# Router rows turned back by TensorE and copied by ScalarE, and a step width summed in PSUM, in a state-space stage

## The chip, the cores and the metric

The kernel runs on one core of a Trainium2 chip. The metric is the device time of one execution in microseconds (us), smaller is better. The core's engines are TensorE (PE, its weight loads are PEld), VectorE (DVE), ScalarE (ACT), GpSimd (POOL) and SyncE (SP, which only issues DMAs). Each engine works through its own program in order; semaphores order the engines among each other. Everything is float32 unless a row says bf16.

## The reference

Two layers over x of shape 2 x 1024 x 128 (2048 rows in all). Layer 0 is adaptive layer norm, a selective state-space block (256 channels, 16 states), a gated residual, a second adaptive norm and a mixture of 8 experts. Layer 1 is the same frame around a gated scan and 16 experts. The change touches the state-space block and the norm behind it:

```python
mod = (_silu(L0_c) @ L0_wmod).reshape(L0_c.shape[0], 6, 1, -1)
sa, ca, ga, sb, cb, gb = (mod[:, 0], mod[:, 1], mod[:, 2], mod[:, 3], mod[:, 4], mod[:, 5])
h = _layernorm(x, axis=-1) * (1 + ca) + sa
...
xc = jax.nn.silu(xc)
x_dbl = jnp.einsum('bld,ed->ble', xc, W_x)
dt, Bm, Cm = jnp.split(x_dbl, [R, R + N], axis=-1)
dt = jax.nn.softplus(jnp.einsum('blr,dr->bld', dt, W_dt) + b_dt)
A = -jnp.exp(A_log)
A_bar = jnp.exp(dt[..., None] * A)
Bu = dt[..., None] * Bm[:, :, None, :] * xc[..., None]
...
_, h_all = jax.lax.associative_scan(comb, (A_bar, Bu), axis=1)
y = jnp.einsum('bldn,bln->bld', h_all, Cm) + D_param * xc
y = y * jax.nn.silu(z)
return jnp.einsum('bld,ed->ble', y, W_out)
...
x = x + ga * _L0_attn_ref(h, ...)
h = _layernorm(x, axis=-1) * (1 + cb) + sb
x = x + gb * _L0_ffn_ref(h, ...)
```

Below, `dt` is called the step width, `dt * xc` is u, the second `h` is "the router's rows": the router scores them and the experts read them from HBM.

## The kernel before, in words

**The stage.** The 2048 positions are cut into 4 chunks of 512 (c = 0 to 3; an even chunk begins a sequence, an odd one goes on from saved carries). Channels are two halves d of 128 partitions. A chunk has 16 steps, one for each state n; step g = 16 c + n. For each step ScalarE writes the decays exp(dt * A) of both halves into PSUM (`decays`), GpSimd multiplies `bu = uT * b` over 128 x 1024 (`inputs`), VectorE runs one scan for each half (`scan`), and the states are multiplied by C into `prod`: of even steps by VectorE (`products`, out of PSUM), of odd steps by GpSimd (`products` of that engine, out of SBUF). TensorE adds `prod` into two PSUM banks with an identity (`add_up`). GpSimd's order is inputs(2k), inputs(2k+1), products(2k-1). `bu` and `prod` are rings of 4 steps, and the B and C rows rings of 3 pairs, which SyncE loads. So for each pair of steps GpSimd has three multiplications, VectorE four scans and one multiplication.

**The work around it** is placed by hand in tables `before` (the next chunk's preparation) and `after` (the chunk behind it), one for each engine, keyed by n, or by the pair m of a chunk for TensorE. For the next chunk: convolution (`conv`, `conv_copy`), `silus`, `low_rows` and `low_and_rows`, `dt_rows`, `dt_parts` and `dt_logs` (softplus in parts: dtT holds relu, a PSUM bank the logarithm), then on VectorE `dt_and_u` at n = 11 and 12, and the z half (`z_half`, `z_copy`). For the chunk behind: `gate_y` at n = 2, `project_out`, `add_x` with its moments at n = 6, `rstd`, `inverse_std` at n = 9 (line 1493), `normed_rows` (ScalarE writes x-hat to `h_tok`), `rows_back` (TensorE turns it into columns), `columns_out` (ScalarE scales and shifts the columns into `hR`), `score_first` (router scores from `hR`), and `router_rows`: at n = 15 VectorE does the same scaling and shifting on the rows themselves, two operations on 128 x 512 (lines 1478 and 1479), for chunks 0, 1 and 2. Chunk 3's rows are done by GpSimd after the stage. `save_rows` (SyncE) writes the rows to HBM.

**Banks.** PSUM bank FRONT serves in turn conv, low rows, the step width of half 0 and z; bank BACK the step width of half 1, the output projection, the turned rows and the scores. FRONT is the bank that the change gives one more use.

The stage spans about 48.7 us (the first `bu`) to 287.6 us. What follows it is the choice of experts and layer 0's experts, then layer 1.

## Time and profile before

| | |
|---|---|
| median of 3 runs (lowest, highest) | 717.08 us (714.65, 719.17) |
| the profiled execution's own time | 712.0 us |
| its span, first to last instruction | 710.2 us |
| mean granted TensorE clock (share of 2.4 GHz) | 0.809 |
| busy share of the span: PE, DVE, ACT, POOL | 64%, 67%, 47%, 58% |

The profile is of one execution; its own time is 5.1 us under the median of the others. Busy shares are means over stages that have different limits, so they say little of one stage: there the rows of each engine in order of time are to be read.

### The profile page before, as it was taken

To read this page: it belongs to the slowest core of one execution; us is meant where nothing else is said; L and a number is where in the kernel's file an instruction comes from. 1 tells how busy PE (TensorE), PEld (TensorE's weight loads), DVE (VectorE), ACT (ScalarE), POOL (GpSimd) and SP (SyncE) were. 2 spreads that over 40 slices of the span, in tenths; PEclk is the share of its full clock that TensorE was granted. 3 is DMA by queue.
4 is the path that set the end of the run, shared out by engine and by line. 5 is a ranking of instruction groups with operands and counts; after the bars stand their busy time and mean duration, and the time that the engine had idled before them with its cause. 6 is when DMAs were issued, how large, how long until landed. Compare 5 with 4: busy or idle time off the path is not lost.

```text
span 710.2 us, 8170 instructions
## 1 busy us (share of the span) xinstructions
PE 456.9 (64%) x2119; PEld 309.4 (44%) x2119; DVE 477.3 (67%) x910; ACT 335.6 (47%) x652; POOL 414.0 (58%) x321
## 2 busy tenths in 40 slices
PE   3655976968787477635878678069640387787520
PEld 2222332423333233524767677025540277776510
DVE  5958899999899999771333223637633747767817
ACT  3164855774586264111222224276320079689805
POOL 0029999999899899216666644421475200645850
PEclk9887999999899799856889989559655589999865
DMA  5053656554344450014666664400011645634125
GB/s 184 0 181 110 182 172 205 176 178 133 119 152 148 134 177 31 15 37 145 197 195 202 194 159 129 122 0 0 16 45 37 208 162 178 212 135 149 42 67 154
DMA packets 58382, 90.21 MB, mean 127 GB/s; under 512 B 7569, under 2 KB 32658, under 8 KB 58338
## 3 DMA queue, kind: packets, MB, share of 16 engines
q1 hardware_dynamic: 51010, 78.36, 34.8%
q0 software_dynamic: 5024, 10.30, 4.7%
q10 hardware_dynamic: 2304, 1.05, 0.5%
q8 instruction: 18, 0.29, 0.2%
q14 instruction: 26, 0.21, 0.1%
HBM read 66.21 MB, written 11.14 MB: 109 GB/s over the span
## 4 chain that ended last, share of the span: by engine, by line
PE 18%; DVE 10%; ACT 10%; issue 7%; another core or an unknown queue 7%; POOL 4%; DMA 3%; ACTq 2%; SPq 1%; DVEq 0%; POOLq 0%
PE ps L1257 5%; PE ps L1246 4%; POOL y_dram L549 2%; PE ps L1415 1%; ACTq L962 1%; PE ps L1297 1%; ACT freq L1002 1%; ACT mag L1000 1%; ACT mag L986 1%; ACT fabs L993 1%; ACT fabs L977 1%; POOL prod L589 1%; PE ps L1086 1%; DMA y_dram<-ys,rows_i 1%
## 5 line engine op out<-in xcount | busy, mean ns | idle before, releaser
L578 POOL TENSOR_TENSOR bu<-uT,b_sb 128x1024 f32<-128x1024 f32 x64 | 151.3, 2386 | 29.5 <-DVE uT L1760 29.5
L549 POOL DMA_INDIRECT y_dram<-ys,rows_i x86 | 92.9, 1080 | 115.9 <-DVE ys L2015 64.2
L1142 PE MATMUL ps<-prod,cst 128*128 128x512 f32 x256 | 128.6, 649 | 39.9 <-DVE yT L1794 16.4
L762 ACT ACTIVATE ps<-dtT,neg_a 128x512 f32<-128x512 f32 x128 | 83.3, 683 | 39.7 <-DVE prod L1784 27.3
L1142 PEld LDWEIGHTS ps<-prod,cst 128*128 128x128 f32 x256 | 50.4, 205 | 109.8 <-issue 75.5
L589 POOL TENSOR_TENSOR prod<-hs,c_sb 128x1024 f32<-128x1024 f32 x32 | 77.7, 2430 | 11.7 <-DVE hs L1774 5.9
L1257 PE MATMUL ps<-w_s,ht 128*128 x312 | 48.6, 305 | 26.2 <-issue 11.0
L859 ACT ACTIVATE ht<-ps,b1T 128x128 f32<-128x128 f32 x78 | 24.5, 368 | 85.9 <-PE ps L1246 48.4
L1257 PEld LDWEIGHTS ps<-w_s,ht 128*128 128x128 f32 x312 | 43.3, 215 | 30.7 <-issue 30.7
L1415 PE MATMUL ps<-xt,mfr 128*128 128x128 f32 x376 | 51.6, 293 | 4.5 <-DVE freq L1978 3.0
L1848 DVE TENSOR_SCALAR ht<-ps,b1T 128x128 f32<-128x128 f32 x78 | 23.8, 346 | 44.8 <-PE ps L1246 26.0
L540 POOL DMA_INDIRECT xl<-h_dram,rows_i x39 | 37.8, 969 | 27.0 <-DVE rows_i L1684 15.4
L1415 PEld LDWEIGHTS ps<-xt,mfr 128*128 128x128 f32 x376 | 48.8, 208 | 6.4 <-issue 4.6
L1246 PE MATMUL ps<-xt,w1r 128*128 128x128 f32 x312 | 48.0, 305 | 1.4 <-issue 1.4
L1246 PEld LDWEIGHTS ps<-xt,w1r 128*128 128x128 f32 x312 | 44.8, 221 | 1.5 <-issue 1.5
L1784 DVE TENSOR_TENSOR prod<-ps,c_sb 128x1024 f32<-128x1024 f32 x32 | 39.2, 1225 | 3.3 <-issue 0.4
L645 POOL DMA_INDIRECT x_slots<-h_tok,slot_i x32 | 32.1, 1004 | 14.3 <-issue 9.8
L1858 DVE TENSOR_TENSOR ys<-ps,b_s 128x128 f32<-128x128 f32 x39 | 11.3, 290 | 42.9 <-remote 19.1
L1116 PE MATMUL ps<-hT,wconv 128*128 128x512 f32 x64 | 34.1, 685 | 9.2 <-ACT zsT L706 8.5
L1774 DVE TENSOR_TENSOR_SCAN ps<-ps,bu 128x512 f32<-128x512 f32 x32 | 37.3, 1210 | 4.1 <-ACT ps L762 4.0
L1774 DVE TENSOR_TENSOR_SCAN ps<-ps,carry,bu 128x512 f32<-128x512 f32 x32 | 39.2, 1270 | 0.6 <-ACT carry L774 0.3
L1774 DVE TENSOR_TENSOR_SCAN hs<-ps,carry,bu 128x512 f32<-128x512 f32 x32 | 39.2, 1266 | 0.1
(289 smaller groups left out, 908.7 us busy)
## 6 DMA issues: line engine op xcount, KB each, us to landing
b_sb<-b_rows SPq DMA_DIRECT2D x32, 512.0 KB
c_sb<-b_rows SPq DMA_DIRECT2D x32, 512.0 KB
mfr<-mf_s SPq DMA_DIRECT2D x47, 256.0 KB
w1r<-in_w SPq DMA_DIRECT2D x39, 256.0 KB
mf_s<-in_mf SPq DMA_DIRECT2D x16, 256.0 KB
xl<-x_slots SPq DMA_DIRECT2D x47, 64.0 KB
w_s<-in_w SPq DMA_DIRECT2D x9, 256.0 KB, 4.8
down_s<-in_down SPq DMA_DIRECT2D x16, 128.0 KB
```

Of the source, the lines that this page charges most:

```text
L540: pool.indirect_dma_start(xl0[:, j % (2 * XR), :], None, h_dram, bass.IndirectOffsetOnAxis(ap=rows_i[:, 0, j:j + 1], axis=0)).then_inc(loa ...
L549: pool.indirect_dma_start(y_dram[l], bass.IndirectOffsetOnAxis(ap=rows_i[:, 1, j:j + 1], axis=0), ys[:, j % slots, :], None).then_inc(save ...
L578: nc.gpsimd.tensor_tensor(bu[:, g % RING, :, :], uT[:, c % 2, :, :], b_sb[:, k % BRING, g % 2, :].unsqueeze(1).broadcast_to([P, ND, CHUNK] ...
L589: nc.gpsimd.tensor_tensor(prod[:, g % RING, :, :], hs[:, k % HRING, :, :], c_sb[:, k % CRING, 1, :].unsqueeze(1).broadcast_to([P, ND, CHUNK]),
L762: nc.scalar.activation(decay_of(g, d), dtT[:, c % 2, d, :], ACT.Exp, scale=neg_a[:, d, n:n + 1]).then_inc(S["a_ready"], 1)
L1116: last = nc.tensor.matmul(bank(conv_bank(c, d)), wconv[:, k, d * P:(d + 1) * P], hT[:, b, lo + k:lo + k + CHUNK], start=k == 0, stop=k == ...
L1142: last = nc.tensor.matmul(bank(Y_BANK + d), ident, prod[:, g % RING, d, :], start=n == 0, stop=n == NS - 1)
L1246: last = nc.tensor.matmul(ps[:, b, at:at + P], w1r[:, j % WR, k * P:(k + 1) * P], xt0[:, j % 2, :], start=True, stop=True)
L1257: last = nc.tensor.matmul(ps[:, 6 + j % 2, 0:C], ht0[:, j % 2, k * P:(k + 1) * P], w2_s[:, bass.ds(e, 1), k, :].rearrange("p a c -> p (a c ...
L1415: last = nc.tensor.matmul(ps[:, b + p % 2 * 2, at:at + P], mfr[:, j % (2 * MR), row:row + P], xt1[:, p % 2, j % 2 * P:(j % 2 + 1) * P], st ...
L1774: nc.vector.tensor_tensor_scan(out, decay_of(g, d), bu[:, g % RING, d, :], carry[:, d, n:n + 1] if c % 2 else 0.0, ALU.mult, ALU.add).then ...
L1784: nc.vector.tensor_tensor(prod[:, g % RING, :, :], even_states(), c_sb[:, k % CRING, 0, :].unsqueeze(1).broadcast_to([P, ND, CHUNK]), ALU. ...
```

## The change

1. **Router's rows.** VectorE's `router_rows` is gone for chunks 0 to 2. In its place TensorE turns `hR` back into rows (`rows_forth`, four transposes into bank FRONT) and ScalarE copies the bank to `h_tok` (a new `router_rows`, one copy of 128 x 512). For chunk 0 this happens in chunk 2 (TensorE at pair m = 2, ScalarE at n = 6), for chunk 1 at the same places of chunk 3, for chunk 2 right after the loop, ahead of the last `project_out`. Waits are added for the bank: TensorE's `low_rows` of chunk 3 waits for the first copy, the last `project_out` for the third, and `columns_out` waits for `rows_ps0` before it overwrites `hR`. SyncE saves the rows of chunks 0 and 1 at n = 14 of chunks 2 and 3 and not at n = 4.
2. **Step width.** In `dt_and_u` the sum goes to the PSUM bank and not to `dtT`, and u is multiplied out of the bank: each of VectorE's two operations then has one operand in SBUF and one in PSUM. ScalarE gets a new `dt_copy` (PSUM to `dtT`, 128 x 512) for each half and chunk: at n = 12 and 13, and two ahead of the first decays. What waited for `dt_ready` because of the bank or because of `dtT` (decays, `z_half`, `project_out`, `rows_back`) now waits for `dt_copied`; GpSimd's `inputs` and ScalarE's `dt_parts` still wait for `dt_ready`.
3. **Small moves.** `z_copy` of half 0 goes from n = 13 to n = 14. Two small loads count on another semaphore.

(The list of semaphore names is left out of the diff.)

```diff
@@ -400,8 +400,8 @@
                 later += [(w2_s[:, es, :, :], w2[:, es, :, :], "in_w1")]
-            later += [(b2_s[:, :, :], b2.partition_broadcast(P), "in_w1"), (nw_s[:, :], norm_w.partition_broadcast(P), "in_nw"),
-                      (rb1_s[:, :], rbias1.partition_broadcast(P), "in_nw"), (b1_r[:, :], b1.rearrange("e (k p) -> (e k) p", p=P), "in_b1"),
+            later += [(b2_s[:, :, :], b2.partition_broadcast(P), "in_w1"), (nw_s[:, :], norm_w.partition_broadcast(P), "in_l1"),
+                      (rb1_s[:, :], rbias1.partition_broadcast(P), "in_l1"), (b1_r[:, :], b1.rearrange("e (k p) -> (e k) p", p=P), "in_b1"),
                       (phase_r[:, :], phase.rearrange("e (k p) -> (e k) p", p=P), "in_b1")]
@@ -431,7 +431,7 @@
                         sp.dma_start(dst, src).then_inc(S[done], 16)
-                    if n == 4 and c >= 2:
+                    if n == 14 and c >= 2:
                         save_rows(c - 2)
@@ -748,11 +748,16 @@
 
+            def dt_copy(c, d):
+
+                act.wait_ge(S["dt_ready"], 2 * c + d + 1)
+                nc.scalar.activation(dtT[:, c % 2, d, :], bank(dt_bank(d)), ACT.Copy).then_inc(S["dt_copied"], 1)
+
             def decays(g):
...
                 if n == 0:
-                    act.wait_ge(S["dt_ready"], 2 * c + 2)
+                    act.wait_ge(S["dt_copied"], 2 * c + 2)
                 for d in range(ND):
@@ -786,11 +791,18 @@
                     act.wait_ge(S["logit_ps"], c)
+                    act.wait_ge(S["rows_ps0"], c)
                 b = c // 2
...
 
+            def router_rows(c):
+
+                act.wait_ge(S["rows_ps0"], c + 1)
+                nc.scalar.activation(h_tok[:, c * CT:(c + 1) * CT, :].rearrange("p t c -> p (t c)"), bank(FRONT), ACT.Copy).then_inc(S["h_ready"], 1)
+
             before = {2: lambda c: conv_copy(c, 0), 4: lambda c: conv_copy(c, 1), 7: low_and_rows, 9: lambda c: dt_parts(c, 0),
-                      11: lambda c: dt_logs(c, 1), 13: lambda c: z_copy(c, 0), 15: lambda c: z_copy(c, 1)}
+                      11: lambda c: dt_logs(c, 1), 12: lambda c: dt_copy(c, 0), 13: lambda c: dt_copy(c, 1), 14: lambda c: z_copy(c, 0),
+                      15: lambda c: z_copy(c, 1)}
             after = {8: lambda c: rstd(1, c), 12: normed_rows, 14: columns_out}
@@ -804,6 +816,8 @@
             columns_first(3)
+            dt_copy(0, 0)
+            dt_copy(0, 1)
             act.wait_ge(S["modT_ps"], 1)
@@ -824,11 +838,14 @@
                     silus(c + 1)
+                if n == 6 and c >= 2:
+                    router_rows(c - 2)
                 if n == 10 and c + 1 < NCHUNK:
...
                     after[n](c - 1)
+            router_rows(NCHUNK - 2)
             after[8](NCHUNK - 1)
@@ -1098,7 +1115,7 @@
                 if d == 0 or c == 0:
-                    pe.wait_ge(S["dt_ready"], 2 * c + d + 1)
+                    pe.wait_ge(S["dt_copied"], 2 * c + d + 1)
                 else:
@@ -1120,6 +1137,8 @@
                 pe.wait_ge(S["xc_ready"], c + 1)
+                if c + 1 == NCHUNK:
+                    pe.wait_ge(S["h_ready"], NCHUNK + 1)
                 for d in range(ND):
@@ -1149,7 +1168,9 @@
                 if c + 1 < NCHUNK:
-                    pe.wait_ge(S["dt_ready"], 2 * c + 4)
+                    pe.wait_ge(S["dt_copied"], 2 * c + 4)
+                else:
+                    pe.wait_ge(S["h_ready"], NCHUNK + c)
                 if c and c + 1 < NCHUNK:
@@ -1162,12 +1183,25 @@
                 if c + 2 < NCHUNK:
-                    pe.wait_ge(S["dt_ready"], 2 * c + 6)
+                    pe.wait_ge(S["dt_copied"], 2 * c + 6)
                 if c + 1 == NCHUNK:
...
                 last.then_inc(S["hT_ps"], 1)
+
+            def rows_forth(c):
+
+                pe.wait_ge(S["hT_sb"], NCHUNK + c + 1)
+                if c == 0:
+                    pe.wait_ge(S["xc_raw"], 2 * NCHUNK)
+                elif c == 1:
+                    pe.wait_ge(S["z_raw"], 2 * NCHUNK)
+                else:
+                    pe.wait_ge(S["h_ready"], NCHUNK + c)
+                for t in range(CT):
+                    last = nc.tensor.transpose(ps[:, FRONT, t * P:(t + 1) * P], hR[:, t * P:(t + 1) * P], ident)
+                last.then_inc(S["rows_ps0"], 1)
 
@@ -1198,6 +1232,8 @@
                     after[m](c - 1)
+                if m == 2 and c >= 2:
+                    rows_forth(c - 2)
                 if m == NS // 2 - 1:
@@ -1215,6 +1251,7 @@
                     score_first(c - 1)
+            rows_forth(NCHUNK - 2)
             project_out(NCHUNK - 1)
@@ -1493,11 +1530,6 @@
 
-            def router_rows(c):
-
-                dve.wait_ge(S["hT_ps"], NCHUNK + c + 1)
-                modulate(c, CB, SB)
-
             def moments(c, done):
@@ -1756,8 +1788,8 @@
                 dve.wait_ge(S["softp_done"], 2 * c + d + 1)
-                then(nc.vector.tensor_tensor(dtT[:, q, d, :], dtT[:, q, d, :], bank(dt_bank(d)), ALU.add))
-                nc.vector.tensor_tensor(uT[:, q, d, :], dtT[:, q, d, :], xcT[:, q, d, :], ALU.mult).then_inc(S["dt_ready"], 1)
+                then(nc.vector.tensor_tensor(bank(dt_bank(d)), dtT[:, q, d, :], bank(dt_bank(d)), ALU.add))
+                nc.vector.tensor_tensor(uT[:, q, d, :], bank(dt_bank(d)), xcT[:, q, d, :], ALU.mult).then_inc(S["dt_ready"], 1)
 
@@ -1803,7 +1835,7 @@
             before = {11: lambda c: dt_and_u(c, 0), 12: lambda c: dt_and_u(c, 1)}
-            after = {2: gate_y, 6: add_x, 9: inverse_std, 15: router_rows}
+            after = {2: gate_y, 6: add_x, 9: inverse_std}
             norm_scale(3)
@@ -1860,7 +1892,7 @@
 
-                dve.wait_ge(S["in_l1"], 32)
+                dve.wait_ge(S["in_l1"], 64)
                 dve.memset(inner_f[:, :], 0.0)
@@ -1945,7 +1977,6 @@
             gated_scan(3)
-            dve.wait_ge(S["in_nw"], 32)
             best_second(0)
```

## Rows read from the trace of the kernel before

**Rows 1.** Busy time of PE, PEld, DVE, ACT, POOL, 46 to 289 us; granted clock, DMA share, GB/s.

```profile
46.00:289.00 243.00, 186.59 (x444) 81.80 (x445) 229.54 (x220) 139.43 (x244) 227.16 (x96) 0.89 0.47 150
```

**Rows 2.** GpSimd's groups of instructions, 48 to 289 us: count, busy us, mean ns, idle before.

```profile
L578 POOL TENSOR_TENSOR bu<-uT,b_sb 128x1024 f32<-128x1024 f32 x64 | 151.3, 2386 | 29.5 <-DVE uT L1760 29.5
L589 POOL TENSOR_TENSOR prod<-hs,c_sb 128x1024 f32<-128x1024 f32 x32 | 77.7, 2430 | 11.7 <-DVE hs L1774 5.9 <-PE ps L1142 4.5 <-DVE ps L1774 1.2
```

**Rows 3.** VectorE's groups of the same stretch.

```profile
L1479 DVE TENSOR_TENSOR h_tok<-h_tok,mod 128x512 f32<-128x512 f32 x3 | 8.1, 2716 | 0.1
...
L1493 DVE SCALAR_TENSOR_TENSOR ln_nmr<-ln_mv,ln_rs 128x4 f32<-128x4 f32 x3 | 4.3, 1441 | 0.0
L1478 DVE TENSOR_TENSOR h_tok<-h_tok,mod 128x512 f32<-128x512 f32 x3 | 4.3, 1438 | 0.0
...
L1794 DVE TENSOR_TENSOR yT<-ps,zsT 128x1024 f32<-128x1024 f32 x3 | 3.6, 1214 | 0.0
```

**Rows 4.** The line of u's multiplication: ns min/median/max, first and last start.

```profile
L1760 DVE TENSOR_TENSOR uT<-dtT,xcT x8: 691/826/2382, 45.4 to 218.5; 128x512 f32<-128x512 f32 x8
```

**Rows 5.** GpSimd in order of time: start, us, line, count, idle before.

```profile
88.48 2.35 POOL L589 TENSOR_TENSOR prod<-hs,c_sb 128x1024 f32<-128x1024 f32 x1
...
95.42 2.79 POOL L589 TENSOR_TENSOR prod<-hs,c_sb 128x1024 f32<-128x1024 f32 x1
98.17 5.10 POOL L578 TENSOR_TENSOR bu<-uT,b_sb 128x1024 f32<-128x1024 f32 x2
...
167.16 2.79 POOL L589 TENSOR_TENSOR prod<-hs,c_sb 128x1024 f32<-128x1024 f32 x1
...
176.44 2.35 POOL L589 TENSOR_TENSOR prod<-hs,c_sb 128x1024 f32<-128x1024 f32 x1 [1.42 <-DVE hs L1774]
...
192.91 2.38 POOL L589 TENSOR_TENSOR prod<-hs,c_sb 128x1024 f32<-128x1024 f32 x1 [2.33 <-PE ps L1142]
...
275.80 4.67 POOL L578 TENSOR_TENSOR bu<-uT,b_sb 128x1024 f32<-128x1024 f32 x2
...
284.89 2.65 POOL L589 TENSOR_TENSOR prod<-hs,c_sb 128x1024 f32<-128x1024 f32 x1 [2.12 <-PE ps L1142]
```

**Rows 6.** VectorE in order of time, first half.

```profile
53.40 2.35 DVE L1774 TENSOR_TENSOR_SCAN ps<-ps,bu 128x512 f32<-128x512 f32 x2
...
84.88 2.33 DVE L1774 TENSOR_TENSOR_SCAN hs<-ps,bu 128x512 f32<-128x512 f32 x2
...
90.68 2.33 DVE L1774 TENSOR_TENSOR_SCAN hs<-ps,bu 128x512 f32<-128x512 f32 x2
...
132.88 0.69 DVE L1800 TENSOR_TENSOR x_tok<-x_tok,ps 128x512 f32<-128x512 f32 x1
...
135.01 2.46 DVE L1774 TENSOR_TENSOR_SCAN hs<-ps,carry,bu 128x512 f32<-128x512 f32 x2
```

**Rows 7.** VectorE in order of time, the end.

```profile
276.27 2.45 DVE L1774 TENSOR_TENSOR_SCAN hs<-ps,carry,bu 128x512 f32<-128x512 f32 x2
...
282.31 2.45 DVE L1774 TENSOR_TENSOR_SCAN hs<-ps,carry,bu 128x512 f32<-128x512 f32 x2
...
293.51 0.69 DVE L1800 TENSOR_TENSOR x_tok<-x_tok,ps 128x512 f32<-128x512 f32 x1
```

**Rows 8.** ScalarE: copies out of PSUM as a group; then in order of time.

```profile
L706 ACT ACTIVATE zsT<-ps 128x512 f32<-128x512 f32 x8 | 4.6, 583 | 0.3 <-PE ps L1105 0.3
...
52.35 2.53 ACT L762 ACTIVATE ps<-dtT,neg_a 128x512 f32<-128x512 f32 x4
...
156.38 1.30 ACT L762 ACTIVATE ps<-dtT,neg_a 128x512 f32<-128x512 f32 x2 [2.16 <-DVE prod L1784]
```

**Rows 9.** TensorE in order of time: start of the stage, of chunk 2, the end.

```profile
48.65 2.08 PE L1105 MATMUL ps<-hT,win_s 128*128 128x512 f32 x2 [0.73 <-DVE uT L1760]
...
181.39 3.75 PE L1142 MATMUL ps<-prod,cst 128*128 128x512 f32 x4 [5.07 <-DVE yT L1794]
...
290.90 2.05 PE L1158 MATMUL ps<-wout_g,yT 128*128 128x128 f32 x16 [0.53 <-DVE yT L1794]
```

More of the change, by code:

```diff
@@ L334, in adaln_two_layers @@
         conv_b, b_dt, d_skip = vec[:, V["convb"]], vec[:, V["bdt"]], vec[:, V["dskip"]]
-        names = ("in_small in_x in_wmod in_ssm in_w1 in_b1 in_l1 in_nw in_down zeros_set h_saved mod_silu mod_ps mod_done "
+        names = ("in_small in_x in_wmod in_ssm in_w1 in_b1 in_l1 in_down zeros_set h_saved mod_silu mod_ps mod_done "
  "consts_b ln_stats ln_rstd h_ready hT_ps hT_sb conv_ps z_ps xc_ready zs_ready dbl_ps dtlow_sb "
- "dt_ps dt_taken softp_done dt_ready bcf_ready b_rows_saved z_raw xc_raw a_ready bu_ready scan_done prod_ready prod_pool "
+ "dt_ps dt_taken softp_done dt_ready dt_copied rows_ps0 bcf_ready b_rows_saved z_raw xc_raw a_ready bu_ready scan_done prod_ready prod_pool "
  "sum_done y_ready o_ps x_added logit_ps logit_sb neg_ready pad_zeroed "
```

## The prediction

> **What bounds the kernel now.** The change touches one stage, so I first read the busy time of each engine in that stretch [rows 1]: of 243 us VectorE is busy 229.5 and GpSimd 227.2, ScalarE 139, TensorE 187. No single engine bounds it: two are at 94%. Which of the two ends a wait is read from GpSimd's groups [rows 2]: 64 multiplications for `bu` and 32 for `prod`, 151.3 + 77.7 = 229.0 us out of the 238.9 between the first start at 48.7 and the last end at 287.5. The rest is 11.7 us of idle time before `prod`: 7.1 for VectorE's scans (5.9 + 1.2), 4.5 put down to TensorE. GpSimd's program is fixed, so the stage ends earlier only if these 11.7 us shrink or its instructions get shorter. Then I read GpSimd in order of time [rows 5]. An unhindered `prod` takes 2.35 us and an unhindered pair of `bu` 4.67; the ones at 95.42 and 98.17 take 2.79 and 5.10, and so does a set of two in each of five places: six of these ten stand where VectorE multiplies u (three chunks), four where it makes the router's rows (167 and 229 us). The last `prod` (2.65) lies beside the third router's rows. The reason is in VectorE's groups: line 1479 takes 2.72 us on average and line 1478 1.44 [rows 3], u's line 691 to 2382 ns [rows 4], while `add_x` of the same size, with one operand in PSUM, takes 0.69 in full GpSimd traffic [rows 6]. So an operation of VectorE with both operands in SBUF waits for GpSimd (up to 2 us) and also holds it up (0.44 each); one with an operand in PSUM does neither.
>
> **The step pair as the unit.** GpSimd needs 6.94 us for a pair of steps (95.42 - 88.48, [rows 5]). VectorE needs 5.80 in an even chunk (90.68 - 84.88, [rows 6]) and 6.04 in an odd one (282.31 - 276.27, [rows 7]). So it wins 1.14 or 0.9 us on GpSimd in each pair, about 9.1 or 7.2 in a chunk of eight, and spends them on extras: `gate_y` 1.2, line 1493 1.4 [rows 3], `add_x` with its moments 2.1 (132.88 to 135.01, [rows 6]), two `dt_and_u` (four operations, at least 2.8), router's rows 1.44 + 2.72 = 4.2. Extras of a full chunk: 12 to 14 us. That is over what it wins, so GpSimd waits: 1.42 us at 176.44, right behind the router's rows [rows 5], and seven times in all beside the one at the start (1.5 of the 5.9 in [rows 2]). After the change the extras are 1.2 + 1.4 + 2.1 + 2.8 = 7.5, about even with what is won: GpSimd becomes the bound nearly throughout.
>
> **Router's rows, removed from VectorE** (three times two operations). GpSimd gets back 4 x 0.44 + 0.30 = 2.05 us of stretching. **u out of PSUM**: six multiplications in the stage (the first chunk's two come before GpSimd starts and take 0.69 already) stretch GpSimd no more: 6 x 0.44 = 2.65. VectorE saves 4.2 for each router's rows and, from the mean of line 1760 against 0.69, some 2.3 over the stage.
>
> **GpSimd's waits, walked through.** Let s be how long before GpSimd needs them VectorE's second scans of a pair are done. At 95.42 it is 95.42 - (90.68 + 2.33) = 2.4. Chunk 0's two `dt_and_u`: 2.4 + 1.14 - 2.8 = 0.7, no wait (0.17 before). Chunk 1: s is 1.9 at its start, gains 0.9 in each of seven pairs, pays 7.5 and about 0.6 for ScalarE, and ends at 0 or a little below by its `dt_and_u`: I keep a wait of 0.3, as before. Then 0.9, and with no router's rows 2.0 at the product of 176.44: the 1.42 is gone and the next 0.2 too. Chunk 2's `dt_and_u`: before them s is 1.1 as in the trace, 1.1 + 1.14 - 2.8 = -0.6, a wait of 0.6 (0.2 before, when stretching hid it). Chunk 3 has no `dt_and_u`: s is 2.0 at its start, its two waits (2.1 together) are gone. Of the seven waits (4.4 us) 0.9 stays: 3.5 gained. The wait at 192.91 (2.33, for TensorE) hangs on `gate_y`: TensorE adds the chunk's first step only then, at 181.39 after 5.07 us idle [rows 9], then a convolution, and 11.5 us later GpSimd may write. `gate_y` now comes 2 us (s) earlier against GpSimd: counted from the product of 176.44, it ends at 2.9 us instead of 4.8; 2.9 + 0.1 + 11.5 = 14.5 against the two pairs that GpSimd has before it, 13.9, leaves 0.6: 1.7 gained. The last wait (2.12 before 284.89) is put down to TensorE, but VectorE's last scan ends at 282.31 + 2.45 = 284.76 too [rows 7]; the last two `bu` end at 280.47 [rows 5], so most of it is the scans' own time; 0.5 is VectorE's lag and goes. Sum: 2.05 + 2.65 + 3.5 + 1.7 + 0.5 = 10.4 us gained on GpSimd's line.
>
> **ScalarE's new work.** Nine copies from here on, and two ahead of the stage, at 583 ns [rows 8]. At n = 12 and 13 it now waits for VectorE's u: by the order of the work, 1.4 us at most, then 0.58. Behind it in the queue is the decay of the next step, which VectorE needs only a scan pair later, and the trace shows 2.16 us idle ahead of it (156.38, [rows 8]); the gap is no smaller in chunks 0 and 2. Cost 0; if the cover were gone, up to 2.0 each. The two router copies at n = 6 stand behind the table loads, where VectorE does wait for ScalarE, but there GpSimd has 0.5 to 1.2 us in hand: 0, at worst 0.6 each.
>
> **The start.** The first two copies stand ahead of the first decays, and TensorE's z halves now wait for them. The second z half starts at 48.65 [rows 9]; now the first one can't start before 48.3, takes 1.75 to 2.08 at this clock, and the second ends some 1.2 us later, and with it the small matmuls and the decays of 52.35 [rows 8]. VectorE's first scan starts at 53.40 [rows 6] with its decay done at 53.0, so 0.4 is covered: 0.8 us lost, all of it on GpSimd's line (bounds 0.3 and 1.6).
>
> **TensorE's new work.** Four transposes at m = 2 in chunks 2 and 3, 0.5 to 1.1 us (sixteen matmuls of that size take 2.05, [rows 9], and twice that at half the clock). Queued behind are two `add_up`, which GpSimd needs 1.6 us or more later: 0. `low_rows` of chunk 3 waits for ScalarE's copy, about when TensorE arrives. `rows_back` waits some 0.6 longer at m = 6, with 3 us in hand behind it. **SyncE** waits for the rows at n = 14 rather than 4: they are long there.
>
> **The end.** Behind the last product: TensorE adds, scores, turns chunk 2's rows (0.6), ScalarE copies (0.6), and only then the projection, which ran at 290.90 after 0.53 idle [rows 9]. It comes 0.6 later, ends at 293.55 instead of 292.95, and VectorE, busy with constants meanwhile, takes it at 293.51 [rows 7]: 0.1 lost (without those constants 0.6). The rows' DMA starts 3 us later than now, 25 us before its first reader.
>
> **A price not in the trace:** VectorE writing a sum into PSUM. The scans that write PSUM take 2.35 a pair and those that write SBUF 2.33 [rows 6], `add_x` with a PSUM operand 0.69. I take 0.69; bounds 0.66 and, as for a scan, 1.2, which over six sums is 3 us of VectorE and perhaps 2 on the line.
> The Trainium skill says otherwise of such operands: "VectorE: DVE Perf Modes", on the TRN2 errata, gives a fixed 120 cycles with a PSUM source against 58 in SBUF. By it each u would cost 65 ns more, 0.4 us over the stage (an estimate from that page); 0.69 for `add_x` against 0.69 for the quickest u shows no such difference.
>
> **Rivals.**
> A. TensorE and ScalarE hold the chunk starts. The transposes, the later z half and a low granted clock after TensorE's idle stretch keep the wait at 192.91 at 2.3 and give another of the kind in chunk 3 (1.5). For it: 5.07 us idle, then 3.75 us for four matmuls [rows 9]. Against: the chain begins with `gate_y`, which comes earlier. 9.5 - 1.7 - 1.5 = 6.3 gained: 710.8.
> B. VectorE's two-operand operations cost GpSimd their whole length and not 0.44. Each of the eleven that leave (six of u, five of the rows) would give back 0.69, 0.25 more than summed: 2.7 us, 704.9. The rows (2.79 against 2.35, [rows 5]) speak against it, unless part of the hold lies outside the durations shown. The Trainium skill has such a rule in "SBUF — State Buffer", on who interferes with whom: with two SBUF inputs against a GpSimd instruction that reads SBUF, the second to issue is blocked until the first is through.
> C. Slower: ScalarE becomes the bound. If its idle gap at n = 12 and 13 is less than the wait for u plus the copy, each of six copies delays a decay, the next scans, u and again ScalarE, by 1.4 + 0.58: 6 x 2.0 = 11.9, and 9.5 - 11.9 is 2.4 us slower than before, 719.5. It decides from a gap under 2.0 us; the trace has 2.16 or more [rows 8], and ScalarE is 57% busy [rows 1]. With the upper bounds of PSUM writes (2), the start (0.8) and the router copies (1.2) it is 723.5.
>
> **How the numbers follow.** 10.4 - 0.8 - 0.1 = 9.5 us. The profiled execution's own time is 712.0 (span 710.2), so 702.5 after; it lies 5.1 below the median of the runs, whose like is 717.08 - 9.5 = 707.6. Chances: forecast 0.62, A 0.20, B 0.06, C 0.08, others 0.04. Range: from B rounded down by the run spread, 703, to past A and toward C, 714. 1% is 7.2 us, about what a measurement of this kernel can tell from no change: the forecast's own spread (705 to 711) lies mostly under 709.9, A and C on the other side; slower by over 1% takes C with its upper bounds and something of the others, 0.05. So 0.66, 0.29, 0.05.
>
> **What would show it.** Right: `prod` and `bu` at 2.35 everywhere in the stage, idle before `prod` near 7 us (11.7 + 0.8 - 5.7), lines 1478 and 1479 gone from VectorE's stage, u at 0.69, stage 229 to 230 us from first `bu` to last `prod`, VectorE with waits for GpSimd. Wrong: a sum over 0.8; `prod` waiting for TensorE over 1 us in chunks 2 or 3; scans waiting for ScalarE at n = 12 to 15; a start more than 1.6 later.

## The result: no gain, and the profile after

| | before | after |
|---|---|---|
| median of 20 runs each (lowest, highest) | 719.09 us (709.51, 729.64) | 719.47 us (715.57, 727.42) |
| profiled execution's own time, span | 712.0, 710.2 us | 718.77, 716.9 us |
| stage, first `bu` to end of last `prod` | 48.68 to 287.54: 238.9 us | 49.51 to 294.97: 245.5 us |
| behind the stage | 422.7 us | 421.9 us |

The ratio after to before is 1.0064, 95% interval 1.0034 to 1.0094. It and the ratios below compare only the executions within 1.5% of each kernel's quickest, which leaves out a part of the executions of the kernel before; the medians and the length of the stage are given beside it for that reason. The forecast was 707.6 us: it was wrong by 12 us and in its sign. All the difference lies in the stage: it is 6.6 us longer, while what stands ahead of it takes 0.8 us more and what stands behind it 0.8 us less.

GpSimd's groups in the stage, 48 to 289 us (it answers to [rows 2]; the last of the 32 `prod` lies outside this window):

```profile
L578 POOL TENSOR_TENSOR bu<-uT,b_sb 128x1024 f32<-128x1024 f32 x64 | 149.4, 2360 | 29.8 <-DVE uT L1792 29.8
L589 POOL TENSOR_TENSOR prod<-hs,c_sb 128x1024 f32<-128x1024 f32 x31 | 73.1, 2359 | 21.2 <-DVE hs L1806 18.6 <-DVE ps L1806 2.5
```

The stretching is gone as forecast (2.36 us each; before 2.39 and 2.43), but the idle time before `prod` has grown from 11.7 to 23.3 us (21.2 here and 2.1 before the last), of it 21.1 for VectorE's scans; the last 2.1 are put down to no engine. VectorE's groups (they answer to [rows 3]) say why:

```profile
L1530 DVE SCALAR_TENSOR_TENSOR ln_nmr<-ln_mv,ln_rs 128x4 f32<-128x4 f32 x3 | 19.8, 6604 | 0.0
L1792 DVE TENSOR_TENSOR uT<-ps,xcT 128x512 f32<-128x512 f32 x7 | 4.8, 691 | 0.2
L1791 DVE TENSOR_TENSOR ps<-dtT,ps 128x512 f32<-128x512 f32 x7 | 4.8, 682 | 1.1 <-ACT ps L749 1.1
```

Line 1530 is line 1493 of the kernel before, unchanged: -mean * 1/std on 128 x 4 numbers, both operands in SBUF. It took 1.44 us on average and now takes 6.60. VectorE and then GpSimd in order of time (start, us) show the two events:

```profile
144.99 9.07 DVE L1530 SCALAR_TENSOR_TENSOR ln_nmr<-ln_mv,ln_rs 128x4 f32<-128x4 f32 x1
153.99 2.45 DVE L1806 TENSOR_TENSOR_SCAN ps<-ps,carry,bu 128x512 f32<-128x512 f32 x2
...
207.94 9.58 DVE L1530 SCALAR_TENSOR_TENSOR ln_nmr<-ln_mv,ln_rs 128x4 f32<-128x4 f32 x1
217.44 2.33 DVE L1806 TENSOR_TENSOR_SCAN ps<-ps,bu 128x512 f32<-128x512 f32 x2
```

```profile
142.46 4.69 POOL L578 TENSOR_TENSOR bu<-uT,b_sb 128x1024 f32<-128x1024 f32 x2
147.07 2.37 POOL L589 TENSOR_TENSOR prod<-hs,c_sb 128x1024 f32<-128x1024 f32 x1
149.37 4.67 POOL L578 TENSOR_TENSOR bu<-uT,b_sb 128x1024 f32<-128x1024 f32 x2
160.25 2.35 POOL L589 TENSOR_TENSOR prod<-hs,c_sb 128x1024 f32<-128x1024 f32 x1 [6.21 <-DVE hs L1806]
...
168.95 2.35 POOL L589 TENSOR_TENSOR prod<-hs,c_sb 128x1024 f32<-128x1024 f32 x1 [1.73 <-DVE hs L1806]
...
223.46 2.36 POOL L589 TENSOR_TENSOR prod<-hs,c_sb 128x1024 f32<-128x1024 f32 x1 [5.97 <-DVE hs L1806]
...
231.92 2.36 POOL L589 TENSOR_TENSOR prod<-hs,c_sb 128x1024 f32<-128x1024 f32 x1 [1.47 <-DVE hs L1806]
```

The instruction begins at 144.99. GpSimd ends one multiplication and begins the next at 147.07, 149.37 and some 2.3 us later, and it isn't served at any of them. It ends at 154.06, just as GpSimd's second `bu` ends (149.37 + 4.67 = 154.04) and GpSimd has nothing it may do: its next `prod` needs a scan that stands behind line 1530 in VectorE's queue. Two scans, a product and two scans later GpSimd goes on, 6.21 us idle. I call this **starvation**: the small instruction is served (it gets through) only when GpSimd stalls, and GpSimd stalls only because of it.

The start of the stage, ScalarE and then VectorE and GpSimd (they answer to [rows 8], [rows 6] and the waits of 1.54 and 1.20 us in the trace of before):

```profile
49.45 0.60 ACT L754 ACTIVATE dtT<-ps 128x512 f32<-128x512 f32 x1 [0.48 <-DVE uT L1792]
54.34 0.17 ACT L822 ACTIVATE modT<-ps 128x4 f32<-128x4 f32 x1 [4.29 <-PE ps L1224]
54.43 2.52 ACT L767 ACTIVATE ps<-dtT,neg_a 128x512 f32<-128x512 f32 x4
```

```profile
55.25 2.35 DVE L1806 TENSOR_TENSOR_SCAN ps<-ps,bu 128x512 f32<-128x512 f32 x2 [1.06 <-ACT ps L767]
```

```profile
61.31 2.35 POOL L589 TENSOR_TENSOR prod<-hs,c_sb 128x1024 f32<-128x1024 f32 x1 [2.57 <-DVE hs L1806]
...
77.74 2.37 POOL L589 TENSOR_TENSOR prod<-hs,c_sb 128x1024 f32<-128x1024 f32 x1 [2.54 <-DVE ps L1806]
```

GpSimd's first two waits are 5.1 us together, 2.4 more than before, where 0.8 was forecast. What ends the second one stands in TensorE's rows, the next chunk's convolution, before and then after:

```profile
60.67 5.12 PE L1116 MATMUL ps<-hT,wconv 128*128 128x512 f32 x8 [8.45 <-ACT zsT L706]
```

```profile
62.52 6.45 PE L1133 MATMUL ps<-hT,wconv 128*128 128x512 f32 x8 [8.22 <-ACT zsT L706]
```

VectorE's scans wait here for decays of ScalarE, and these stand in ScalarE's queue behind the copy of the convolution. The same eight matmuls take 1.33 us longer after the change because TensorE's granted clock goes from 1.2 to 2.4 GHz later within them: its mean over them is 0.71 of full speed before and 0.57 after.

### The profile page after: what moved, and what is told of

It is laid out like the page before. It is cut to its first block, busy times and chain, and to the rows that moved or that the text cites. A ratio compares the mean times of both kernels' runs of the same rounds, so it can differ in the third digit from the quotient of the medians.

```text
span 716.9 us, 8203 instructions
## 1 busy us (share of the span) xinstructions
PE 457.0 (64%) x2131; PEld 310.8 (43%) x2131; DVE 476.9 (67%) x904; ACT 341.0 (48%) x663; POOL 409.7 (57%) x321
## 4 chain that ended last, share of the span: by engine, by line
PE 17%; issue 12%; DVE 7%; POOL 7%; ACT 4%; another core or an unknown queue 4%; DMA 3%; SPq 2%; ACTq 2%; POOLq 0%; DVEq 0%
POOL y_dram L549 5%; PE ps L1294 5%; PE ps L1283 5%; PE ps L1334 2%; ACTq L979 1%; SPq L503 1%; DMA y1b<-y_dram 1%; PE ps L1103 1%; DMA y_dram<-ys,rows_i 1%; ACT h_tok L898 1%; PE ps L1326 1%; DVE ht L1880 1%; PE ps L1342 1%; PE ps L1363 1%
## 5 line engine op out<-in xcount | busy, mean ns | idle before, releaser
L578 POOL TENSOR_TENSOR bu<-uT,b_sb 128x1024 f32<-128x1024 f32 x64 | 149.4, 2360 | 29.8 <-DVE uT L1792 29.8
L1161 PE MATMUL ps<-prod,cst 128*128 128x512 f32 x256 | 125.7, 637 | 44.6 <-DVE prod L1816 29.4
L589 POOL TENSOR_TENSOR prod<-hs,c_sb 128x1024 f32<-128x1024 f32 x32 | 75.5, 2359 | 23.3 <-DVE hs L1806 18.6
L1294 PE MATMUL ps<-w_s,ht 128*128 x312 | 47.1, 298 | 26.1 <-issue 13.1
```

The source lines that it names most:

```text
L578: nc.gpsimd.tensor_tensor(bu[:, g % RING, :, :], uT[:, c % 2, :, :], b_sb[:, k % BRING, g % 2, :].unsqueeze(1).broadcast_to([P, ND, CHUNK] ...
L589: nc.gpsimd.tensor_tensor(prod[:, g % RING, :, :], hs[:, k % HRING, :, :], c_sb[:, k % CRING, 1, :].unsqueeze(1).broadcast_to([P, ND, CHUNK]),
L1161: last = nc.tensor.matmul(bank(Y_BANK + d), ident, prod[:, g % RING, d, :], start=n == 0, stop=n == NS - 1)
L1294: last = nc.tensor.matmul(ps[:, 6 + j % 2, 0:C], ht0[:, j % 2, k * P:(k + 1) * P], w2_s[:, bass.ds(e, 1), k, :].rearrange("p a c -> p (a c ...
```

## The experiments

Eighteen runs followed, two of them of the two kernels as they are. The stage's length in the profiled execution is the measure that tells most: it doesn't hold what the rest of the kernel does from one execution to the next. Each length in the table is that of one execution.

| kernel | stage, us | instructions of 5 us or more on VectorE with two SBUF operands |
|---|---|---|
| before (712.0) | 238.9 | none |
| before, profiled again | 243.3 | 7.95 |
| before_split; before_drain | 238.6; 239.5 | none |
| after; after, profiled again | 245.5; 246.7 | 9.07, 9.58; 9.09, 9.57 |
| after_split | 229.3 | none |
| after_drain; after_mid2 | 230.2; 230.2 | none |
| after_near_far; after_far_near | 240.2; 237.1 | 9.57; 9.07 |
| after_mid | 247.3 | 9.10, 9.58 |
| after_yield; after_split_start | 231.7; 229.7 | none |
| after_n10; after_wide | 239.2; 253.2 | 5.46, 5.64; 9.13, 9.63, 8.63 |
| part1; part2 | 255.4; 245.3 | 9.06, 9.58, 8.95; 9.11 |
| part1_split; part2_split | 236.7; 241.3 | 10.07; 9.14 |

**First group: both kernels profiled again, and line 1530 in another form.** The edit, on both kernels (after_split, before_split):

```diff
-                nc.vector.scalar_tensor_tensor(out=ln_nmr[:, c, :], in0=ln_mv[:, c, :, 0], scalar=-1.0, in1=ln_rs[:, c, :],
-                                               op0=ALU.mult, op1=ALU.mult).then_inc(S["rs1"], 1)
+                for t in range(CT):
+                    ins = nc.vector.tensor_scalar(ln_nmr[:, c, t:t + 1], ln_mv[:, c, t, 0:1], ln_rs[:, c, t:t + 1], -1.0, ALU.mult, ALU.mult)
+                ins.then_inc(S["rs1"], 1)
```

> The kernel before, unchanged, profiled once more. Theory 1 (starvation: the 4-element line 1493, which has two operands in SBUF, now and then finds no gap in GpSimd's instructions; the first profile of before was a lucky one): line 1493 takes 1.2 to 1.8 us in a run near 710 and 6 us or more at least once in a run near 720 or over. Theory 2 (only the changed kernel has this): it takes under 2 us all three times, whatever the run's time.

> The changed kernel, profiled once more. Theory 1: line 1530 (the same instruction) takes over 6 us in one to three of the three chunks, and the time moves by about 7 us with each. Theory 2 (fixed by the order of work): the same two chunks as in the first profile, 9.1 and 9.6 us. Theory 3 (the loss is ScalarE's copies): scans wait for ScalarE at n = 12 to 15.

> The changed kernel with line 1530 made of four one-column multiplications, each with one SBUF tensor and one per-partition scalar. Theory 1 and 2: none of them takes over 0.3 us, the two idle times of GpSimd of 6 us are gone, and the time is 7 to 10 us (1.0 to 1.4%) under before. Theory 3 (ScalarE's copies or TensorE's waits are the loss and the long instruction only shows it): the same time as the changed kernel, within 2 us.

> The kernel before with the same replacement. Theory 1: if before is starved too in many of its runs, it gains more than the 1.2 to 1.8 us that its profile shows: 3 to 8 us, and its runs scatter less. Theory 2 (only the changed kernel is starved): 0 to 2 us faster.

Measured beside a median of 718.56 us for the kernel before: after_split 703.31 us (699.17 to 706.09), ratio 0.9849 (0.9787 to 0.991); before_split 712.76 us, ratio 0.9982 (0.9935 to 1.0029). The second profile of the kernel after (720.37 us) repeats both events at the same places. Without the two-operand form the stage takes 229.3 us, where the forecast was 229 to 230; GpSimd's groups are

```profile
L578 POOL TENSOR_TENSOR bu<-uT,b_sb 128x1024 f32<-128x1024 f32 x64 | 149.2, 2353 | 29.2 <-DVE uT L1793 29.2
L589 POOL TENSOR_TENSOR prod<-hs,c_sb 128x1024 f32<-128x1024 f32 x32 | 75.3, 2354 | 7.2 <-DVE hs L1807 3.2 <-DVE ps L1807 2.2 <-issue 1.7
```

so 4.5 us less busy and 4.5 us less idle than before. The gain is larger than the 7 to 10 us expected of this run: by the ratio some 11 us. In the kernel before the same edit changes neither the stage (238.6 us against 238.9) nor the ratio clear of noise; its median is 5.8 us lower, which may be a starvation less often, but no profile shows it. And the second profile of the kernel before (713.56 us) held a surprise that neither of its theories had, since line 1493 took 1.1 to 1.8 us in all three chunks. VectorE first, then GpSimd:

```profile
211.29 7.95 DVE L1760 TENSOR_TENSOR uT<-dtT,xcT 128x512 f32<-128x512 f32 x1
```

```profile
226.51 2.35 POOL L589 TENSOR_TENSOR prod<-hs,c_sb 128x1024 f32<-128x1024 f32 x1 [7.82 <-DVE hs L1774]
```

The kernel before is starved too in some executions, there by u. The profile that the prediction was read from had none.

**Second group: the kind of instruction, its place, and the other side.** All times of this group are shorter (before 674.99 us), and not through the stage: after_split_start's is as long as after_split's, and 379.6 us lie behind it where after_split has 421.3. Why is not known, so only ratios and stages are compared with the other groups. after_yield: GpSimd waits for line 1530 before it begins the product of n = 9. after_wide: after_split and, behind it, one multiplication of 128 x 512 with two SBUF operands whose result nobody reads. after_n10: line 1530 one step later. after_split_start: after_split, and chunk 0's step width and u in the old form, without ScalarE's two copies.

```diff
+                if g % NS == 9 and g > NS:                                   # after_yield, GpSimd's products
+                    pool.wait_ge(S["rs1"], g // NS)
+                if c + 1 < NCHUNK:                                           # after_wide
+                    nc.vector.tensor_tensor(wide_s[:, :], xcT[:, c % 2, 0, :], uT[:, c % 2, 0, :], ALU.mult)
-            after = {2: gate_y, 6: add_x, 9: inverse_std}
+            after = {2: gate_y, 6: add_x, 10: inverse_std}                   # after_n10
```

> The changed kernel with line 1530 as it is, but in chunks 1 to 3 GpSimd's product of n = 9 also waits for its result, so GpSimd must leave a gap once. Starvation theory: the instruction ends with GpSimd's running multiplication, within 2.4 us in each chunk; GpSimd loses at most 0.5 us each time; the time is 6 to 9 us below the changed kernel, near after_split. Rival (the instruction is slow for another reason, such as its operands or ScalarE's writing of ln_rs beside it): still about 9 us in chunks 1 and 2, and the time is not under the changed kernel's.

> after_split plus, behind the four small ones in each chunk, one multiplication of 128x512 with both operands in SBUF into a scratch (work that nobody uses). If any operation with two SBUF operands can be starved once GpSimd has no gaps, it takes over 6 us at least once. If only the 4-element instruction is affected, it takes 0.7 to 2.8 us each time, as lines 1478 and 1479 did before.

> The changed kernel with line 1530 moved from n = 9 to n = 10, which changes only when it asks against GpSimd's instructions. If starvation hangs on GpSimd having no gap alone, it is starved in the same chunks (over 6 us). If it hangs on the moment of asking, some chunk changes: one that was starved takes under 2.4 us, or chunk 3's is starved.

> after_split, and chunk 0's step width in the old form (sum in SBUF, no copy by ScalarE, z halves wait for VectorE's u as before). GpSimd's first two waits fall back from 2.6 and 2.2 to 1.5 and 1.2 us; 2 us below after_split. If the late start was covered later, the same as after_split within 1 us.

Measured: after_yield 661.38 us, ratio 0.9856 (0.9762 to 0.9949), line 1530 at 2.20, 2.67, 1.16 us: a pause of GpSimd, with VectorE's instruction left as it is, brings the gain. after_wide 681.3 us: the larger operation waits 9.13, 9.63 and 8.63 us, so size isn't what matters, and such an instruction brings the starvation back. after_n10 667.0 us: 5.46, 5.64, 2.10 us; VectorE is less far ahead there, GpSimd runs dry sooner, and the wait is shorter: it ends with GpSimd's stall, not after a fixed time. after_split_start 657.87 us, ratio 0.9793 (0.9719 to 0.9868): GpSimd's first wait is back at 1.54 us, so the copies of chunk 0 cost 1.0 us there; its second is 2.67 and not 1.20, the convolution taking 6.58 us, and the stage is 229.7 us, no shorter than after_split's, where 2 us less were expected. The quickest ratio of all, but its interval holds after_split's.

**Third group: what decides whether it is served.** GpSimd's instructions normally overlap by 0.03 to 0.08 us; I call it a gap where one begins at or after the end of the last, by the hundredths that the rows show. In the traces so far most served instructions had their last gap at most 9 GpSimd instructions back, some u's of a second half 11, and starved ones 12 to 28. So I put gaps in: GpSimd waits on the count that its own last product raises, ahead of pair k.

```diff
             for k in range(PAIRS):
+                if k in (12, 17):           # after_near_far; (9, 20) after_far_near; (10, 18) after_mid; (11, 19) after_mid2
+                    pool.wait_ge(S["prod_pool"], k - 1)     # (12, 20, 28) after_drain
                 inputs(2 * k)
```

> The kernel after, with line 1530 kept, and with GpSimd made to wait twice for its own last product before it goes on (one wait on a count that GpSimd itself raises): once 5 to 6 of its instructions before line 1530 of chunk 1, once 14 to 15 before that of chunk 2. Such a wait empties GpSimd's pipeline and costs some 0.1 us. Theory (VectorE's two-operand instruction is served between two GpSimd instructions only if GpSimd's last gap lies at most about 9 instructions back; the traces so far have hits at 2 to 9, misses at 12 to 27): line 1530 takes 1.1 to 2.7 us in chunk 1, with no wait of 6 us on GpSimd behind it, and 8 to 10 us in chunk 2, with a wait near 6 us. The time is that of the kernel after less one starvation, 7 to 8 us. Rival 1 (phase or chance decides, not the gap): 9 us in both chunks, as in both traces of the kernel after. Rival 2 (any gap since the last starvation will do): about 2 us in both.

> As the run before with the two distances exchanged: GpSimd waits for its own last product 14 to 15 instructions before line 1530 of chunk 1, and 5 to 6 before that of chunk 2. Theory: 8 to 10 us in chunk 1 and 1.1 to 2.7 us in chunk 2, the mirror image. If chunk 1 is quick in both or slow in both, the distance isn't what decides.

Measured: 713.09 and 715.85 us, one execution each, beside a median of 721.69 for the kernel before. Both came out as the theory had it, mirrored. Line 1530 (line 1532 here) in after_near_far, then in after_far_near:

```profile
143.75 2.31 DVE L1532 SCALAR_TENSOR_TENSOR ln_nmr<-ln_mv,ln_rs 128x4 f32<-128x4 f32 x1
...
200.11 9.57 DVE L1532 SCALAR_TENSOR_TENSOR ln_nmr<-ln_mv,ln_rs 128x4 f32<-128x4 f32 x1
```

```profile
142.42 9.07 DVE L1532 SCALAR_TENSOR_TENSOR ln_nmr<-ln_mv,ln_rs 128x4 f32<-128x4 f32 x1
...
205.38 0.47 DVE L1532 SCALAR_TENSOR_TENSOR ln_nmr<-ln_mv,ln_rs 128x4 f32<-128x4 f32 x1
```

Such a gap is 0.08 us wide in the trace. **The parts alone** belong to the same group: part1 is the router's rows with the old step width, part2 the step width with the old rows (each is the diff above without the other half).

> The first part of the change alone: router's rows by TensorE and ScalarE, step width and u as in the kernel before. By the prediction's own terms this gives back 2.05 us of stretching, most of the waits behind the router's rows (1.6) and part of the wait at the start of chunk 2, 4 to 6 us, with no cost at the start: 0.992 to 0.995 of before. By the theory of the gaps, GpSimd's gaps behind the router's rows of chunk 1 (1.4, 0.2, 2.3 us) are what lets line 1493 in at chunk 2; without them the last gap lies 17 or more instructions back and line 1493 takes 8 to 10 us in chunk 2, and about 1.8 in chunk 1, where nothing has changed ahead of it: 7.7 us lost, so 1.00 to 1.005 of before. Rival (only the step width part brings the starvation): line 1493 under 2.7 us in all chunks and 0.992 to 0.995.

> The second part alone: step width summed in PSUM, u from there, ScalarE's copies; router's rows by VectorE as before. Prediction's terms: 2.65 us of stretching given back, waits about the same, 0.8 lost at the start (2.4 as the trace of after shows it): 0 to 2 us quicker, 0.997 to 1.000. By the theory of the gaps chunk 0 has then no gap after its start, so line 1493 of chunk 1 comes 25 or more instructions behind the last one and takes 8 to 10 us; in chunks 2 and 3 it comes 6 to 9 behind the gaps that the router's rows cause and takes under 2.7: 7.7 us lost once, 1.006 to 1.012 of before.

part1: 721.17 us (710.26 to 739.53), ratio 0.9981 (0.9885 to 1.0077), before 721.69. The interval holds both what the theory and what the rival gave, so the trace decides; and there the profiled execution (731.37) had three starved instructions where I expected one: the small gap near 131 us on which I had counted in chunk 1 wasn't there (the last one lay 18 instructions back). In the five traces that have this gap, all with the old step width, GpSimd's second wait at the start was 1.2 to 1.3 us; in part1 it was 2.6, behind a convolution of 6.55 us. part2: 719.66 us, ratio 1.0058 (0.9984 to 1.0131), which can't be told from no change either; one starved instruction, in chunk 1, and served ones of 1.41 and 1.17 us behind the gaps that the router's rows make: as expected. So neither part shows the gain alone, and by these traces each takes away some of the gaps by which the remaining two-operand instructions were served.

**Fourth group: the border, a cure without touching VectorE, the parts without line 1493.** part1_split and part2_split are part1 and part2 with the edit of after_split.

> The kernel after, GpSimd made to wait for its own last product once about 11 of its instructions before line 1530 of chunk 1, and once about 10 before that of chunk 2. Counted over the eleven traces so far, every two-operand instruction of VectorE that began with GpSimd's last gap 1 to 11 instructions back took 0.5 to 2.7 us, and every one at 12 or more (12, 13, 14, 17 to 30) took 5.5 to 9.6. Theory with the border between 11 and 12: both under 2.8 us, GpSimd without a wait near 6 us, time as the kernel after less 15 us. Rival (the chance of being served falls off gradually, so that 10 and 11 are luck): at least one of them 8 us or more.

> The kernel after, GpSimd waiting for its own last product once in each of chunks 1, 2 and 3, 4 to 6 instructions before line 1530; nothing changed on VectorE. Theory: line 1530 under 2.8 us in all three, no wait near 6 us on GpSimd, and the gain that the kernel with line 1530 in four one-column instructions showed (0.985), less at most 1 us for line 1530 itself and the three drains: 0.984 to 0.989 of before. Rival (a gap only moves the starvation to another place, or the drains cost GpSimd more than 0.3 us each): 0.995 or more.

> Router's rows by TensorE and ScalarE alone, with line 1493 in four one-column instructions; u still has two operands in SBUF. Prediction's terms for the rows: 2.05 us of stretching, 1.6 us of waits behind the rows of chunk 1, up to 1.7 at the chunk's start, 2.1 in chunk 3: 6 to 7 us quicker than the kernel before without starvation (712), 0.990 to 0.992. If u (two operands, six times in the stage) is itself starved now that the rows' gaps are gone, as it was once in a run of the kernel before, one u takes 8 to 10 us and the ratio is 1.00. By the count: u of chunk 1 comes at 9 and 11 behind the small gap of 131 us if that gap is there, and u of chunk 2 at 20 or more behind the last one, so I expect one starved u, in chunk 2, and 0.998 to 1.003.

> Step width in PSUM alone, with line 1493 in four one-column instructions; router's rows by VectorE. Prediction's terms: 2.65 us of stretching given back, 1.9 us lost at the start (4.8 us of first waits against 2.9), other waits as before: about 1 us quicker than the kernel before without starvation, 0.995 to 1.000 of before. The rows' instructions have two SBUF operands and come right behind GpSimd's wait at the start of chunk 2 in chunk 1's case only if that gap is there; otherwise they come 30 instructions behind the last gap and starve: then 8 us at the first rows, and 1.005 to 1.012.

after_mid went against the theory: 9.10 and 9.58 us at 11 and 10 instructions (726.86 us, one execution). after_drain, with 0.08 us gaps 4 to 5 instructions ahead, has the whole gain: 703.63 us (700.25 to 709.05), ratio 0.9879 (0.9837 to 0.9921):

```profile
141.66 2.31 DVE L1532 SCALAR_TENSOR_TENSOR ln_nmr<-ln_mv,ln_rs 128x4 f32<-128x4 f32 x1
...
197.87 0.48 DVE L1532 SCALAR_TENSOR_TENSOR ln_nmr<-ln_mv,ln_rs 128x4 f32<-128x4 f32 x1
```

```profile
158.86 2.35 POOL L589 TENSOR_TENSOR prod<-hs,c_sb 128x1024 f32<-128x1024 f32 x1 [1.05 <-DVE hs L1808]
```

part1_split: 723.18 us, ratio 1.0168 (1.0075 to 1.0261), four runs only. Its stage is 236.7 us with one starved u in chunk 2 (10.07 us, last gap 20 instructions back), as expected; but the ratio lies far above the 0.998 to 1.003 expected. Its other three executions (721.44 to 725.65 us) were slower than the profiled one (715.82), and what they held isn't seen. part2_split: 715.45 us, ratio 1.0028 (0.9976 to 1.008); it is the router's rows that starve here, 39 instructions behind the last gap, as its expectation allowed, at a ratio somewhat under the 1.005 to 1.012 that it gave for this case:

```profile
165.01 9.14 DVE L1504 TENSOR_TENSOR h_tok<-h_tok,mod 128x512 f32<-128x512 f32 x1
174.19 0.69 DVE L1505 TENSOR_TENSOR h_tok<-h_tok,mod 128x512 f32<-128x512 f32 x1
```

**Fifth group: the border again, and the kernel before with gaps.** before_drain has the same wait ahead of pairs 4, 6, 12, 14, 20, 22, 28 and 30.

> As the run with the gaps 11 and 10 instructions ahead of line 1530, but now 8 in chunk 1 and 7 in chunk 2 (16 to 20 us). If the border lies between 9 and 10 instructions (19 to 21 us served, 22.8 us and more not), line 1530 takes under 2.8 us in both, and GpSimd has no wait near 6 us: 15 us less than the kernel after. Rival (a gap made by GpSimd's wait for itself works less far than one made by a wait for another engine, only 4 to 6 instructions): 9 us in at least one.

> The kernel before, with GpSimd waiting for its own last product twice in each chunk, at n = 8 and n = 12, so that line 1493, u and the router's rows all come within some 9 instructions of a gap. If the 20 us between the quickest and the slowest execution of the kernel before is starvation that comes in some executions and not in others, the highest time falls under 718 and the median to 709 to 713 (the profiled runs without starvation are at 712.0), 0.987 to 0.992 of before; the rest of the distance to 703 is then what the change itself is worth. Rival (the scatter has another source): the same spread of 15 us or more and a ratio of 0.997 to 1.004.

after_mid2, 8 and 7 instructions: 2.20 and 0.36 us, 704.59 us (one execution), stage 230.2. before_drain: median 710.64 us (703.52 to 713.81) beside 717.66 (705.46 to 724.39) for the kernel before. The median and the highest are as expected. The ratio, 1.0018 (0.9962 to 1.0073), lies outside the 0.987 to 0.992 expected, while the medians give 0.990; the stage of the profiled execution, 239.5 us, is no shorter than before.

## Why the prediction was wrong, by its own steps

**The step that failed** is in "the step pair as the unit": of the extras, "line 1493 1.4" was carried over unchanged, and from the sum of the extras it followed that "GpSimd becomes the bound nearly throughout". The second is what happened, and it is what made the first untrue. While GpSimd waited now and then, line 1493 was served at the next boundary between two of its instructions. The change removed the waits and the stretching, GpSimd ran 27 and 17 instructions without a gap (30 in place of 27, if a boundary near 84.7 us where two just touch isn't counted), and the unchanged instruction took 9.07 and 9.58 us. The stage would be 229.3 us (after_split) and is 245.5: two events, 8.1 us each. I had read that such an operation waits "up to 2 us" and charged only its cost to GpSimd, never asking what it would find once GpSimd had no idle time left.

**The Trainium skill** was read too narrowly in the same way. "SBUF — State Buffer", in its summary of rules, has the second to issue blocked until the first is through; I weighed that as rival B, a price on GpSimd. The traces agree on who blocks whom: line 1530 began at 144.99, behind a GpSimd instruction begun at 144.77. They differ on the length: the block lasted over three further instructions of GpSimd, until GpSimd stalled.

**Terms that held**, measured in after_split, where nothing is starved: GpSimd busy 229.0 to 224.5, 4.5 gained (4.7 forecast), so 0.44 for each stretching was right; rival B would have given 7.4 and was wrong. u and its sum take 0.69 and 0.68 us. The waits other than the first two fell from 9.0 to 2.4, 6.6 gained (5.7 forecast: 3.5 + 1.7 + 0.5). The wait at 192.91 is gone, and the longest wait put down to TensorE in any trace with both parts of the change is 0.9 us: rival A wrong, though the low granted clock that it names did cost time, at the start of the stage (below). ScalarE waits 0.5 us in all for u ahead of its eight copies, and the copies take 0.59 each. So rival C was wrong, and that the time came out beside its 719.5 is chance. The last projection waits 0.69 us for ScalarE's copy and VectorE 0.23 for it: 0.1 forecast. The stage without starvation is 9.6 us shorter than before, as forecast (10.4 - 0.8), but in part by luck: the waits gave 0.9 more than forecast, GpSimd's busy time, overlaps counted once (227.2 to 222.1), 0.4 more, and the start took 1.3 more away.

**The term that was mis-sized** is the start: 0.8 forecast, 2.4 in the trace of after (2.1 in after_split). 1.0 of it is the two copies, by after_split_start and part1, whose first waits are 1.54 and 1.53. The rest is the second wait, 1.20 before, which the prediction read past and put into no term. It goes with TensorE's convolution. Where its eight matmuls take 5.11 to 5.26 us (mean granted clock 0.70 to 0.72), the wait is 1.2 to 1.3; where they take 6.06 to 6.58 (0.55 to 0.60), it is 2.1 to 2.7. All traces with the new step width throughout are of the second kind. But so is part1, and it runs the same instructions up to this point as part1_split, which is of the first kind (2.62 against 1.19 us): the later rise of the clock isn't tied to the step width alone, and what sets its moment stays open.

**The base.** The profile of before stood 5.1 us under the median, which I took as a constant. In good part it is not: with gaps put in, the median is 7.0 us lower. Against that (710.64), after_drain's 703.63 and after_split's 703.31 are some 7 us lower. These come from other groups; set against the kernel before beside each, they are 15 to 16 us lower, which would leave 8 to 9 for the change itself, and the stages (239.5 against 230.2 and 229.3) say 9 to 10. So the change is worth 7 to 10 us once nothing is starved.

**What is shown and what isn't.** Shown by taking it away and putting it back: the 9 us are a two-operand instruction of VectorE that GpSimd doesn't let in; a gap of 0.08 us at most 8 instructions earlier lets it in, one 10 or more earlier doesn't. The border rests on one execution at each distance. Over all traces, where GpSimd was running, nearly 80 such instructions had the gap 1 to 9 instructions back and took 0.36 to 2.72 us, and 20 had it 10 to 39 back and took 5.46 to 10.07; three more (15 to 27 back, 2.20 to 2.67 us) were let in when GpSimd had to wait for something else. Seven u's of a second half came at 11 (25.6 us) and were served; each stood one or two instructions behind one of GpSimd's that the first half had stretched. That this let them in is an explanation found afterwards, which no run tested. Why a gap works that far, and whether instructions or time count (20.6 us served, 22.8 not, these u's aside), isn't known. That starvation is all of the scatter of the kernel before is argued from one profile and one set of ten runs; nothing profiled one of its long executions.

## What to carry to other kernels

When an edit makes a neighbour engine run without pause, look again at every instruction that shares something with it, the unchanged ones too: a mean duration read while the neighbour still had idle time isn't a price. Here the cure costs little: keep VectorE from two SBUF operands (four one-column instructions, 0.55 us in all, in place of one), or let GpSimd wait once for itself shortly before (0.08 us). Read a second profile of the kernel before if its runs scatter by 20 us, since one profile shows one of its ways to run.

## What the runs showed of the hardware that was not expected

- A VectorE instruction with two SBUF operands, of 128 x 4 or of 128 x 512, takes up to 10.07 us beside back-to-back GpSimd multiplications, of which three or four begin meanwhile (two in after_n10). It ends with GpSimd's stall: the small one 0.02 us behind it (154.06 against 154.04), the large one 0.55 us behind it. The small one takes 0.16 us when GpSimd is idle.
- A wait of GpSimd for its own last instruction opens 0.08 us, and that is enough for an instruction that comes up to 8 of GpSimd's later.
- Four `tensor_scalar` with one-column operands in SBUF take 0.55 us together beside GpSimd at full load; in six kernels none took over 0.21 us in the stage.
- VectorE's sum into PSUM takes 0.68 us, as much as into SBUF.
- The same eight matmuls take 5.1 or 6.5 us in two kernels that are the same up to there (part1_split, part1), as TensorE's granted clock rises from 1.2 to 2.4 GHz sooner or later within them. Here that moves GpSimd's wait by 1.4 us.
